# Inverse row sums spread over the context's layout by one transfer of 256 KB instead of four of 64 KB

## What is computed

```python
# layer 0: layernorm, attention (A), output projection, residual;
#          layernorm, cross attention (B), output projection, residual;
#          layernorm, MLP of 4*512 with gelu, residual
# layer 1: cross attention (D) on a layernormed context, gated, residual
def attention(q, k, v, mask):             # 16 heads of 32
    scores = jnp.einsum('bhqd,bhkd->bhqk', q, k) / jnp.sqrt(jnp.float32(HD))
    scores = scores * mask - 10000.0 * (1.0 - mask)
    probs = jax.nn.softmax(scores, axis=-1)
    return jnp.einsum('bhqk,bhkd->bhqd', probs, v)
```

## Time and profile before

| | |
|---|---|
| median of three runs | 1096.29 us |
| lowest, highest | 1094.27, 1097.34 us |
| the profiled execution's own time | 1095.73 us |
| its span in the trace | 1094.2 us |
| granted TensorE clock over the span | 1.0 |
| TensorE busy | 1065.7 us, 97% of the span |
| data moved by transfers | 185.92 MB in 145831 packets |
| TensorE busy in 240 to 300, 360 to 420 and 420 to 510 us | 60.00, 58.49 and 86.55 us |

### The profile page before, as it was taken

How to read it: one execution, slowest core, us unless ns; L and a number is a source line. 1 busy time by engine, 2 the same in 40 slices (tenths; PEclk the granted TensorE clock), 3 DMA queues, 4 the chain that set the end, 5 groups by cost and what they waited for, 6 DMA issues and landing times.

```text
span 1094.2 us, 24221 instructions
## 1 busy us (share of the span) xinstructions
PE 1065.7 (97%) x8741; PEld 924.8 (85%) x8741; DVE 819.2 (75%) x1299; ACT 703.2 (64%) x2354; POOL 482.8 (44%) x361
## 2 busy tenths in 40 slices
PE   7989999999999999999999999999999999999998
PEld 6888888888888888887898888888888988888886
DVE  6678787778888788978867667767697466666767
ACT  4687777777888878787444444444455276666676
POOL 3665665657767766767613122114032222222210
PEclk9999999999999999999999999999999999999999
DMA  6366666577777677564253251341648636666621
GB/s 217 98 194 204 197 194 192 175 213 218 214 229 236 201 222 240 158 192 155 77 147 101 72 173 47 127 130 68 207 134 263 219 128 203 207 212 205 198 69 60
DMA packets 145831, 185.92 MB, mean 170 GB/s; under 512 B 17856, under 2 KB 88752, under 8 KB 145712
## 3 DMA queue, kind: packets, MB, share of 16 engines
q1 hardware_dynamic: 145712, 184.37, 53.6%
HBM read 122.59 MB, written 61.73 MB: 168 GB/s over the span
## 4 chain that ended last, share of the span: by engine, by line
PE 52%; DVE 13%; ACT 10%; DMA 7%; POOL 6%; issue 5%; SPq 4%; DVEq 0%; ACTq 0%; POOLq 0%
PE psum L1089 15%; PE psum L1070 14%; PE psum L892 10%; POOL prob L2204 6%; PE psum L1009 4%; PE psum L884 4%; ACT prob L1374 4%; ACT prob_blocks L1374 3%; DVE ln_tile L1689 2%; DMA normalised<-ln_tile 2%; DVE prob L1754 2%; DVE negmax L1767 2%; DMA ln_tile<-stream 2%; PE psum L910 2%; ACT inputs_transposed L1412 1%
## 5 line engine op out<-in xcount | busy, mean ns | idle before, releaser
L892 PE MATMUL psum<-inputs_hi,weights_hi 128*128 128x256 f32 x768 | 223.6, 291 | 4.7 <-POOL inputs_lo L2190 2.5
L892 PE MATMUL psum<-inputs_lo,weights_hi 128*128 128x256 f32 x768 | 217.1, 283 | 0.0
L892 PE MATMUL psum<-inputs_hi,weights_lo 128*128 128x256 f32 x768 | 217.0, 282 | 0.0
L2204 POOL TENSOR_TENSOR prob<-prob,mask_bias 128x1024 f32<-128x1024 f32 x64 | 152.7, 2407 | 99.4 <-DVE prob L1754 97.4
L892 PEld LDWEIGHTS psum<-inputs_hi,weights_hi 128*128 128x128 f32 x768 | 146.7, 191 | 10.1 <-issue 2.8
L1767 DVE TENSOR_REDUCE negmax<-prob 128x8 f32<-128x1024 f32 x96 | 115.7, 1212 | 50.1 <-POOL prob L2204 49.9
L1374 ACT ACTIVATE prob<-prob,negmax 128x128 f32<-128x128 f32 x384 | 148.3, 391 | 0.4 <-DVE negmax L1767 0.4
L892 PEld LDWEIGHTS psum<-inputs_lo,weights_hi 128*128 128x128 f32 x768 | 147.0, 191 | 0.2
L892 PEld LDWEIGHTS psum<-inputs_hi,weights_lo 128*128 128x128 f32 x768 | 146.9, 191 | 0.0
L2190 POOL TENSOR_TENSOR inputs_lo<-inputs_transposed,inputs_hi 128x512 fp32r<-128x512 f32 x70 | 93.0, 1349 | 94.4 <-DVE inputs_hi L1727 61.9
L1374 ACT ACTIVATE prob_blocks<-prob,negmax 128x128 f32<-128x128 f32 x304 | 117.5, 389 | 23.9 <-DVE negmax L1767 23.7
(11 more groups left out here) (132 smaller groups left out, 2654.0 us busy)
## 6 DMA issues: line engine op xcount, KB each, us to landing
prob_turned<-prob_blocks SPq DMA_DIRECT2D x38, 512.0 KB, 3.0
prob<-prob_turned SPq DMA_DIRECT2D x152, 128.0 KB, 3.3
weights_whole<-weights_in SPq DMA_DIRECT2D x72, 256.0 KB, 3.4
inputs_transposed<-normalised SPq DMA_DIRECT2D x120, 128.0 KB, 2.8
normalised<-ln_tile SPq DMA_DIRECT2D x24, 512.0 KB, 2.8
context<-row_sums_spread SPq DMA_DIRECT2D x188, 64.0 KB, 2.1
stream<-residual SPq DMA_DIRECT2D x42, 256.0 KB, 2.9
ln_tile<-stream SPq DMA_DIRECT2D x32, 256.0 KB, 3.9
```

The lines of the kernel that those rows point to most:

```text
L892: mm = pe.matmul(ps[:, bank, GT * part:GT * part + GT], w[:, slot, c, o], a[:, buf, c, :], start=c == 0 and i == 0, stop=c == KC - 1 and i ...
L2204: pool.tensor_tensor(half, half, mb.unsqueeze(1).to_broadcast([128, 8, T]), ALU.add).then_inc(s_biased, 1)
```

## The change

The four transfers of `spread_row_sums`, each of one row to 32 partitions, become one. Its destination is the whole tile; its source is written out as an access pattern: four rows, each repeated 32 times (stride 0), 512 values. It adds 16 to the semaphore, and the two waits on `s_rsp` count by 16 instead of 64. Nothing else is changed. It is done in all 47 items that have a spread.

```diff
@@ -668,7 +668,7 @@
             def store_row_sums(g):
                 sp.wait_ge(s_rc, g + 1)
                 if g:
-                    sp.wait_ge(s_rsp, 64 * g)
+                    sp.wait_ge(s_rsp, 16 * g)
                 sp.dma_start(spread.rearrange("j (c n) -> (j c) n", c=KC), rsumT[:, :]).then_inc(s_rst, 16)
 
             def spread_row_sums(g):
@@ -676,8 +676,8 @@
                 sp.wait_ge(s_rst, 16 * (g + 1))
                 if g:
                     sp.wait_ge(s_clo, 2 * g)
-                for j in range(4):
-                    sp.dma_start(ctxn[32 * j:32 * j + 32, :], spread[j:j + 1, :].to_broadcast([32, KC * T])).then_inc(s_rsp, 16)
+                each = bass.AP(spread.tensor, spread.offset, [[KC * T, 4], [0, 32], [1, KC * T]])
+                sp.dma_start(ctxn[:, :], each).then_inc(s_rsp, 16)
 
             def load_stream(g):
                 load_residual(g % 2, g // 2, g // 16, g % 16)
@@ -1792,7 +1792,7 @@
             def context(g, h):
                 half = slice(256 * h, 256 * h + 256)
                 dve.wait_ge(s_pv, 4 * g + (4 if value_bank(g, 1) == T_BANK else 2 * h + 2))
-                dve.wait_ge(s_rsp, 64 * (g + 1))
+                dve.wait_ge(s_rsp, 16 * (g + 1))
                 dve.tensor_tensor(ctxn[:, half], ps[:, value_bank(g, h), half], ctxn[:, half], ALU.mult).then_inc(s_cx, 1)
```

## The result

The changed kernel takes 1101.94 us, the median of 5 runs (1099.95 to 1105.03), and the kernel before 1096.29 (1094.27 to 1097.34). The ratio is 1.0054 with a 95% interval of 1.0033 to 1.0076: slower by 3.6 to 8.3 us. The profiled execution has a span of 1099.5 us against 1094.2, so it shows 5.3 of these microseconds.

A forecast was written before the change was run, and what follows sets the result against it. TensorE was taken as busy for 97% of the span, with 48% of the end set by other work. Attention B's 4.8 us and the end's 3.6 made 8.4 us on 1095.73, plus 0.56: 1104.7 us; range 1095.5 to 1116.

The forecast's parts named there:

- the likeliest case: Spread on four engines lands after 5.2 us; VectorE's waits in tight items bring the time to 1104.7 us; chance 0.55.
- delay without consequence: Rival: four engines, but attention B's waits vanish in slack between engines, leaving the end's 3.6 us: 1099 us; chance 0.12.
- upper bound: Spread landing after 6.9 us: up to 1.7 us more at each of seven places, 12 in all, about 1116 us.
- Part 1, the issues removed: SyncE queue: three issues fewer in each of 47 items, 65 us of SyncE in sum, next to none on the path.
- Part 2, the landing: Spread's transfer: four source rows keep it on four engines, 64 KB each, landing after 5.2 us instead of 3.4.
- the signs named beforehand: Changed profile: landing near 5.2 us; VectorE waits in some ten items, was two; L949 waits more; attention A, items 32-41 unchanged.
- Part 3, attention B: Items 14, 17, 21 and 23: delays reaching the end of 1.1, 1.7, 0.4 and 1.6 us, 4.8 in sum.
- hold-up of 1.0 us: Item 17: four issues took 2.74 us instead of 1.71, so the new landing was put at 6.2 us.
- Part 3, the end: Items 42 to 46: 0.9 us at 42, 0.7 at 44, 0.4 at 45, 1.6 at 46; 3.6 in sum.
- All 16 engines: Rival: engines share the transfer by its destination's 128 rows, landing after 2.7 to 3.4 us: 1094.5 us; chance 0.13.
- Pile-up behind the spread: Rival: transfers issued behind the spread find four engines busy, about 8 us on top: 1113 us; chance 0.20.

The follow-up runs named there:

- the run on 16 engines: Changed kernel with its one transfer reading row 0 repeated 128 times, rows 1 to 3 left out: 1094.46 us, ratio 0.9984 to the kernel before.
- The runs with 2, 4 and 16 rows: Changed kernel with two transfers of 2 rows each, 1189.76 us; as it is, 1101.94; with 16 source rows, each inverse sum written four times, 1102.78.
- the run of items 0 to 31: Kernel before with the joined transfer in items 0 to 31 only, four transfers in the others: 1097.51 us, ratio 1.0012.
- the run of items 32 to 46: Kernel before with the joined transfer in items 32 to 46 only, four transfers in the others: 1100.37 us, ratio 1.0036.
- the covered items: Kernel before with the joined transfer only in items 0 to 13 and 27 to 41, whose issue-to-use distance was long: 1095.92 us, ratio 0.9993.

## Why the prediction was right, and where its terms were off

**Sign and size.** 1104.7 us was forecast, 1101.94 measured, slower by more than 0.3% as the likeliest case had it. Of the excess of 8.4 us that the sum gave, 5.7 came (5.3 in the span of the profiled execution). The measured time is as near to the rival *delay without consequence* (1099) as to the forecast, so the mechanism is judged by the runs below and not by this number. One slip in the upper bound: the sum has eight places, not seven, and 1.7 us at each make 13.6, not 12.

**Part 1, the issues removed.** They were to be worth next to nothing on the path, and that nearly holds: the run on 16 engines puts their worth at about 1.8 us, and most of the rest went into SyncE's waits for VectorE. A small term was missing: the one issue takes 0.54 us, 0.12 more than one of the four, since the trace of before had no such pattern.

**Part 2, the landing.** The step that carried the argument was right. Four engines at work show as a share of 0.25. Item 43 and item 46, where VectorE was there early, were to be at 5.3; they came out at 5.1 and 4.7. The engines move 25 GB/s each when only four work, not the 19.6 of the run's mean, which makes 0.7 us for 64 KB, and so the 0.6 us at item 46. By the rule of the Trainium skill, page "DMA: Bandwidth & Descriptors", section "Rules for kernel authors", the outermost dimension sets the number of engines. The runs with 2, 4 and 16 rows agree with it: at item 46 the multiplication starts 8.0 and 4.7 us behind the first issue with 2 and 4 rows, and with 16 rows the landing comes after 3.4. What I didn't have is that the landing grows with what is issued behind it: 5.8 us in item 14, 6.3 in item 42 and 6.5 in item 40 against 4.7 in item 46. A likely reason is that the later transfers' packets share the four engines with the spread's; it is read from the order of issues alone, and no run tests it.

Of the signs named beforehand, the waits of VectorE came in 13 items: 14, 15, 17, 19, 21, 25, 26, 40 and 42 to 46. Item 23, named among the first, isn't one of them, and item 40 lies in the stretch that was to stay unchanged.

**Part 3, attention B: 4.8 us forecast, about 1.3 found (-0.1 to 2.7 by the run of items 0 to 31).** Three of the four waits are where they were to be, but the sum was too high. The single items below are read from one pair of traces, and are no surer than that:

- Item 14: VectorE waits 1.53 us (1.8 forecast). ScalarE did wait 0.95 us for the context, but TensorE's transposition stands at 266.93, 0.9 us ahead of before, as far as the kernel was ahead anyway: nothing was lost, where 1.1 was forecast. That isn't so in every execution: in the trace with items 0 to 31 joined the same item waited 2.81 us, and TensorE stood 1.1 us further back by item 16. The forecast let the delay of ScalarE pass on to the end because what follows it is on the chain somewhere; in the second trace the spread was issued 0.6 us later against the rest of the program and took 0.3 us longer, and it did.
- Item 17: 1.01 us of waiting and some 0.5 lost, where 1.7 was forecast. I had carried the queue's hold-up of 1.0 us over to the new landing. It doesn't stand before the spread any more: the one issue takes 0.54 us and starts 0.5 us earlier against the rest of the program, and the landing is at 5.6, not 6.2. A part of the hold-up now falls on the mask's issue, the second behind the spread, which took 0.43 us before:

```profile
305.46 1.10 SPq L662 DMA_DIRECT2D mask<-mask_b_in  x1
```

- Item 21: VectorE waits 0.62 us. TensorE's wait went from 0.93 to 0.38. Nothing was lost, 0.4 was forecast.
- Item 23: no wait, 1.6 forecast. The issue is at 393.24 instead of 394.15, 0.8 us earlier against the rest of the program, and the landing came less than 5.8 us behind it, not 6.6: the hold-up of 1.4 us that I had added is gone, and no issue behind the spread is long.

VectorE also waits in items 15, 19, 25 and 26, which I hadn't priced, 0.55, 1.06, 0.48 and 0.93 us, and the traces put the loss between items 17 and 20 and between 25 and 28, with gains of 0.5 and 0.9 at items 21 and 23 between them. So the step that failed in attention B has two parts. At the two items with a busy queue the sum added the old hold-up, 2.4 us in all, to the new landing, though it stood between the removed issues and not before them. And the other terms took VectorE's waits for losses of the whole, where in the run of items 0 to 31 8.9 us of waiting cost 1.3.

**Part 3, the end: 3.6 us forecast, 3.3 found in the trace, 4.0 by the run of items 32 to 46.** The sum came out by luck; its terms did not. Item 42 cost 2.0 instead of 0.9, since its landing took 6.3 us and TensorE waited 1.85 us for `rtotal` there. Item 43 cost nothing and item 44 0.7, both as forecast (VectorE had waited 1.99 us for item 43's spread before the change too), item 45 nothing (0.4 forecast), and item 46 only 0.6 instead of 1.6, since its landing took 4.6 and VectorE still had other work for 4.2 us. The trace of the kernel with items 32 to 46 joined has the same three places, with 1.4, 0.4 and 0.6 us. TensorE's wait at L949 over the run rose from 6.0 to 9.6 us:

```profile
L949 PE MATMUL psum<-identity,rtotal 128*16 128x128 f32 x47 | 12.8, 273 | 9.6 <-DVE rtotal L1775 9.6
```

**The stretch from item 28 to 42: nothing forecast, 1.6 us in the trace.** Item 40 waits for its landing in this stretch, but only for 0.49 us. The run with the joined transfer in the covered items doesn't confirm a loss (0.9993, up to 1.0011, or 1.2 us), and the trace of the kernel on 16 engines goes from 0.6 us behind at item 30 to 3.3 at item 31 though its runs are no slower than before. It stays open.

**The rivals.** *All 16 engines* was priced at 1094.5 us, and the run that forces it gave 1094.46. *Delay without consequence* was priced at 1099: it was right on attention B, where its reason holds (8.9 us of waits cost 1.3), and the measured time lies between it and the forecast. I had given it too little. *Pile-up behind the spread* was half seen. The masks' landing rose from 2.5 to 5.1 us in attention B and from 3.2 to 5.5 in the last stage. The weights' landing, right behind the spread, grew from 3.4 us to the value in this row of the issues after (count, KB each, median us to landing), and the inputs of the last stage from 3.3 to 5.0:

```profile
weights_whole<-weights_in SPq DMA_DIRECT2D x72, 256.0 KB, 5.3
```

The transfers that I had named as its victims, the normalised tiles and the encoder's inputs, stayed at 2.9 and 5.0 us (2.8 and 4.9 before); they are issued later. No engine waits longer for the ones that were hit. So the mechanism is real, and no cost of it was found here; what the covered items leave room for is 1.2 us.

## What to carry to other kernels

Joining transfers is only a gain if the joined one still spreads over all engines: look at the outermost dimension of its pattern, and read the cut from the DMA share behind one lonely issue. Then compare the new landing with the time from issue to use in every item, since only the tight ones pay, and there one item can pay more than all the rest. And where an edit takes issues out of a queue, don't carry a hold-up seen between them over to the new issue: it may go away or fall on an issue behind it.

## What the runs showed of the hardware that I had not expected

- Two transfers with 2 rows each, issued one behind the other, used the same two engines: 8.0 us to the landing of both, where two pairs of engines would have given about 5, at a DMA share of 0.13.
- An issue on SyncE takes 0.34 us (a row repeated 128 times), 0.42 (32 times, four issues running) or 0.54 (three-dimensional source). From memory to memory it is 0.50 (row repeated 96 times) or 0.63 (four rows, each repeated 24 times).
- Four engines alone reach about 100 GB/s, 25 each, and two 51; the mean of a busy engine over the run is 19.6.
- A transfer on four engines landed after 4.6 us when nothing was issued close behind it, and after 6.2 to 6.4 us with a mask and four loads behind it.
- 9 MB more of traffic on all 16 engines, 5% of the whole, cost 11 us, 1% of the time, though the engines are busy for only 54% of the span. Forty-seven more issues without the bytes cost 2 (0.5 to 3.8).
